# Nine buffers of widened counts in place of six, and a quarter of GpSimd's descriptor ring, in a three-layer graph network on one Trainium2 core

## The chip, the cores and the metric

The kernel runs on one core of one Trainium2 chip. The metric is the device time of one execution in microseconds (us). The kernel before takes 7069.22 us, the median of three runs (7048.0 to 7079.48).

## What is computed

12500 nodes of 128 features, 200000 edges sorted by destination. The first layer is a gated one: messages of the source nodes plus an embedding of the edge's type are summed at their destinations, and a GRU cell updates the nodes. Three layers follow in which each node sums its neighbours' rows and encoded edge attributes, and a two-layer perceptron with a batch norm turns the sums. Each half ends in a layer norm of the residual.

```python
def _gin_layer(x, ei, ea, p, concat):
    enc_w, enc_b, w1, b1, g, be, rm, rv, w2, b2 = p
    ee = ea @ enc_w + enc_b
    src = x[ei[1]]
    h = jnp.concatenate([src, ee], axis=1) if concat else src + ee
    agg = jax.ops.segment_sum(h, ei[0], num_segments=x.shape[0])
    h = agg @ w1 + b1
    h = jax.nn.relu(_bn_eval(h, g, be, rm, rv))
    return h @ w2 + b2
...
x = _layernorm(x + _L0_gnn_ref(x, edge_index, edge_type_9, ...), axis=-1)
x = _layernorm(x + _L1_gnn_ref(x, edge_index, edge_attr_16, ...), axis=-1)
```

`_L1_gnn_ref` calls `_gin_layer` three times, with a self loop added for every node.

## The kernel before, in words

The program has three stages, one after the other, on five queues that its author wrote out by hand: TensorE, VectorE, ScalarE, GpSimd and SP (which issues the plain DMAs). There is no scheduler. Each instruction waits for a count on a semaphore, and each engine takes its instructions in the order in which they are written.

**Sorting and counting.** The edges are ranked and written to memory in a new order by 1563 scatters of GpSimd (L3017, one DMA of 128 records each). For the destinations in groups of 512 and the first 60 blocks of 128 source nodes (60 is `BD`), one-hot matrices are multiplied into matrices of counts: how many edges lead from source s to destination d. The counts are bytes and lie in memory (`counts`).

**First layer.** It has counted blocks and gathered blocks; 611 gathers of GpSimd fetch rows (L3033), into 16 buffers (`QR`) of four tiles each. Its output goes to memory in two forms, as dense parts (for the counted blocks) and as rows to gather.

**Three layers.** 25 groups of 512 destinations in each, so 75 groups k (`SG` is 25; the last group of nodes has 256). The 60 counted source blocks of a group are taken in 30 steps (`HALF`) of two blocks each. For a step:

- SP loads counts, two steps at a time, 256 KB into one of five buffers of `MS` (`MR` = 5, L3248). Before it reuses a buffer, it waits until both widenings of it are done.
- ScalarE (L2575) or, every third step, VectorE (L2258) widens 128x1024 bytes to 32-bit floats in one of `RM` buffers of `MSR`. Before that it waits until the step that used this buffer before has been multiplied (`m_used`, a semaphore that TensorE raises with the last matmul of a step). The widening of step g is written four steps ahead (`AH` = 4) of step g's place in these engines' programs.
- TensorE (L2965) does four matmuls: two blocks, each with a high and a low part of the node features (`HP`), against the widened counts, and adds all into one PSUM bank. It waits for the step's widening.

The sources that aren't counted are gathered: GpSimd fetches their rows (L3051) into six buffers of `GL`, VectorE makes one-hots (L2239), TensorE sums (L2935), VectorE adds three parts up (L2276, L2269) and TensorE turns the result (L2880, L2884). There are 28 gathers in a group. Between the steps of group k stand the perceptron's pieces for group k - 1 (L2899 to L2914 on TensorE, L2295 and L2302 on VectorE, L2610 to L2638 on ScalarE), and SP loads and stores what they need. At the end of a layer, SP reloads `HP` in pieces of 2 MB, 2 MB, 3 MB and 0.5 MB (L3251), and the count loads of the next group stand behind these in its queue.

What the change touches are the number of buffers `RM`, with the waits and the index in L2256 to L2259, L2573 to L2576 and L2965, and the size of the area in which GpSimd's DMAs (L3017, L3033, L3051) keep their descriptors. The tensors start behind that area. The wait of a widening is

```python
            if g >= RM:
                s.wait_ge(m_used.sem, g - RM + 1)
```

Of the kernel before, what the change touches and what calls it, by code (L numbers as in the profile page):

```python
# [48 lines left out]
BD = 4 * J  # L49
HALF = 2 * J  # L50
MR = 5
RM = 6
AH = 4
HB = [0, 16, 32, BD - 4, BD]
NQ0 = (C + GT - 1) // GT
# [1503 lines left out]
def program(nc, x, dst, src, typ, ea, wmsgT, wihT, whhT, emb, bmsg, bih, bhh, encT, w1a, w1b, w2, pv, out):  # L1559
    ctx = ExitStack()  # L1560
    with ctx:
        def sb(name, shape, dt=F32, into=ctx):
            return into.enter_context(nc.sbuf_tensor(name, shape, dt))
# [154 lines left out]
        MS = sb("MS", [P, MR, 1024], BF16, layers)  # L1718
        MSR = sb("MSR", [P, RM, 2, 512], F32R, layers)
        GL = sb("GL", [P, LR, LT, 448], BF16, layers)  # L1720
# [531 lines left out]
        def widen_vector(v, g):  # L2252

            i, w = g // 2, GRP[g // HALF].w
            v.wait_ge(m_in[i % MR].sem, 16 * (i // MR + 1))
            if g >= RM:  # L2256
                v.wait_ge(m_used.sem, g - RM + 1)
            v.tensor_copy(MSR[:, g % RM, :, 0:w].rearrange("p t (c s) -> p t c s", s=P),  # L2258
                          MSB[:, i % MR, 0:4 * w].rearrange("p (c h s t) -> p h t c s", h=2, s=P, t=2)[:, g % 2]).then_inc(*wide_dve.inc())  # L2259
# [309 lines left out]
        def widen_scalar(s, g):  # L2569

            i, w = g // 2, GRP[g // HALF].w
            s.wait_ge(m_in[i % MR].sem, 16 * (i // MR + 1))
            if g >= RM:  # L2573
                s.wait_ge(m_used.sem, g - RM + 1)
            s.copy(MSR[:, g % RM, :, 0:w].rearrange("p t (c s) -> p t c s", s=P),  # L2575
# [884 lines left out]
```

## Time and profile before

| | us |
|---|---|
| median of 3 runs | 7069.22 |
| lowest, highest run | 7048.0, 7079.48 |
| span of the profiled execution | 6981.5 |
| TensorE busy in it | 5386.3 (77%) |
| GpSimd busy | 4213.9 (60%) |
| VectorE busy | 3769.9 (54%) |
| ScalarE busy | 3302.5 (47%) |

The profile is of one execution. For this one only the span, from the first to the last instruction, is listed; what lies around it is not. An engine's busy time is the union of its instructions; a matmul's end is modelled, its start is recorded. The granted clock is TensorE's as a share of the full one. "Idle before" is the time for which an engine did nothing just before an instruction, put down to what ended it; "remote" and "another core or an unknown queue" are waits for which the profile found no releaser, "issue" is time in which it saw no wait.

### The profile page before, as it was taken

How to read it: one execution, taken by the hardware profiler on the slowest of the kernel's cores; microseconds unless marked ns; L12 is line 12 of the kernel's file. 1: busy time of each engine (PE TensorE's matmuls, PEld its weight loads, DVE VectorE, ACT ScalarE, POOL GpSimd, SP SyncE). 2: the span in 40 equal slices, each digit the busy share in tenths (PEclk: the TensorE clock that was granted, in tenths of full speed). 3: DMA queues.
4: the chain of work that ended last, by engine and by line, in shares of the span. 5: the costliest groups of instructions: out<-in, count | busy, mean ns of one | idle time of the engine just before them, and what ended most of it. 6: DMA issues, size and time to landing. Idle time of an engine off the chain costs nothing.

```text
span 6981.5 us, 88118 instructions
## 1 busy us (share of the span) xinstructions
PE 5386.3 (77%) x26429; PEld 3361.9 (48%) x26429; DVE 3769.9 (54%) x14165; ACT 3302.5 (47%) x4432; POOL 4213.9 (60%) x4243
## 2 busy tenths in 40 slices
PE   4376767676766764666676999999898998898998
PEld 1133333333333322333344666666666666666666
DVE  8576767777766754455566444443333333444443
ACT  1164545555655641122122666665555554554554
POOL 5655555555555556666631666666676666666665
PEclk5588988888988985677776999999999999999999
DMA  7165556556655652333323666667666667666665
GB/s 250 48 144 129 140 121 138 127 134 136 157 127 127 148 138 76 98 101 102 100 78 121 188 190 185 194 196 220 184 186 179 190 191 217 184 184 174 177 185 148
DMA packets 1068177, 1066.40 MB, mean 153 GB/s; under 512 B 494051, under 2 KB 784501, under 8 KB 1067701
## 3 DMA queue, kind: packets, MB, share of 16 engines
q1 hardware_dynamic: 889573, 782.05, 40.1%
q0 software_dynamic: 178128, 278.65, 16.0%
q8 instruction: 220, 3.60, 0.2%
q14 instruction: 256, 2.10, 0.1%
HBM read 747.21 MB, written 216.68 MB: 138 GB/s over the span
## 4 chain that ended last, share of the span: by engine, by line
PE 44%; another core or an unknown queue 6%; DVE 4%; issue 4%; ACT 2%; DMA 1%; SPq 0%; DVEq 0%; ACTq 0%
PE ps L2965 27%; PE ps L2935 4%; PE ps L2848 2%; PE ps L2899 2%; PE ps L2809 2%; PE ps L2810 1%; DVE BIG L2197 1%; PE ps L2909 1%; PE ps L2910 1%; PE ps L2811 1%; ACT MSR L2575 1%; DVE MSR L2258 0%; PE ps L2812 0%; PE ps L2914 0%
## 5 line engine op out<-in xcount | busy, mean ns | idle before, releaser
L3051 POOL DMA_INDIRECT GL<-h_gathered,IDXA x2058 | 2112.6, 1027 | 1227.7 <-issue 568.5
L2965 PE MATMUL ps<-MSR,HP 128*128 128x512 f32 (+1 forms) x9000 | 2375.0, 410 | 174.9 <-ACT MSR L2575 71.2
L3017 POOL DMA_INDIRECT rec_q<-BIG x1563 | 1513.7, 968 | 1156.2 <-issue 473.6
L2575 ACT CAST MSR<-MS 128x1024 fp32r<-128x1024 uint8 (+1 forms) x1500 | 1491.8, 1028 | 1272.9 <-PE ps L2965 820.3
L2965 PEld LDWEIGHTS ps<-MSR,HP 128*128 128x128 f32 x9000 | 1675.6, 195 | 624.9 <-issue 168.5
L2750 PE MATMUL ps<-MTB,XPS 128*128 128x512 bf16 x4410 | 1312.2, 416 | 1.1 <-DMA XPS<-x_parts 0.8
L2258 DVE CAST MSR<-MS 128x1024 fp32r<-128x1024 uint8 (+1 forms) x750 | 522.6, 699 | 1236.7 <-PE ps L2965 738.5
L2457 ACT CAST MT<-ps 128x512 uint16<-128x512 f32 x735 | 427.4, 582 | 959.2 <-remote 633.3
L2461 ACT CAST MTB<-MT 128x1024 bf16<-128x1024 uint8 x735 | 767.9, 1045 | 64.8 <-PE ps L2750 10.3
L3033 POOL DMA_INDIRECT BIG<-x_parts,SRCq x611 | 582.8, 954 | 341.5 <-issue 164.4
L2750 PEld LDWEIGHTS ps<-MTB,XPS 128*128 128x128 bf16 x4410 | 439.7, 103 | 248.7 <-issue 68.1
L2935 PE MATMUL ps<-GL,SL 128*128 128x384 bf16 (+1 forms) x2058 | 456.0, 338 | 8.9 <-issue 7.3
L2709 PE MATMUL ps<-BIG 128*128 128x392 f16 x435 | 165.2, 380 | 354.4 <-DVE BIG L2052 269.1
L2733 PE MATMUL ps<-BIG 128*128 128x256 bf16 x738 | 215.5, 293 | 286.8 <-DVE BIG L2034 83.7
L2034 DVE TENSOR_SCALAR BIG<-I,BIG 128x258 bf16<-128x258 f16 x982 | 335.0, 399 | 188.3 <-remote 162.5
L2197 DVE TENSOR_SCALAR BIG<-IO,DREL 128x256 bf16<-128x256 f16 x1579 | 352.7, 299 | 94.2 <-remote 84.6
L2239 DVE TENSOR_SCALAR SL<-IOTH,RELA 128x128 bf16<-128x128 f16 x2058 | 387.1, 263 | 0.0
L1976 DVE TENSOR_SCALAR BIG<-IOTM,BIG 128x98 f16<-128x98 f16 x1804 | 346.5, 254 | 0.0
L2809 PE MATMUL ps<-WE,BIG 10*128 10x512 f32 x196 | 166.3, 940 | 197.7 <-ACT XMT L2522 158.8
L2052 DVE CAST BIG<-ps 128x98 f16<-128x98 f32 x435 | 109.6, 252 | 306.9 <-remote 288.0
L2733 PEld LDWEIGHTS ps<-BIG 128*128 128x128 bf16 x738 | 77.6, 105 | 395.7 <-issue 179.7
L2935 PEld LDWEIGHTS ps<-GL,SL 128*128 128x128 bf16 x2058 | 154.7, 98 | 229.3 <-issue 166.2
(248 smaller groups left out, 6244.4 us busy)
## 6 DMA issues: line engine op xcount, KB each, us to landing
MS<-counts SPq DMA_DIRECT2D x1080, 256.0 KB
counts<-BIG SPq DMA_DIRECT2D x360, 256.0 KB
XPS<-x_parts SPq DMA_DIRECT2D x192, 384.0 KB
GL<-h_gathered,IDXA POOLq DMA_INDIRECT x2058
rec_q<-BIG POOLq DMA_INDIRECT x1563
rec_q<-BIG SPq DMA_DIRECT2D x44, 490.0 KB, 10.4
HTI<-h_cols SPq DMA_DIRECT2D x72, 256.0 KB
h_dense<-PCL SPq DMA_DIRECT2D x30, 512.0 KB
```

Source lines behind the costliest of these rows:

```text
L2197: got = v.tensor_scalar(hot[:, i, :], IO256[:, :], DREL[:, GT * q + i:GT * q + i + 1], None, ALU.is_equal)
L2239: got = v.tensor_scalar(SL[:, r % LR, i, :], IOTH[:, :], RELA[:, q + i:q + i + 1], None, ALU.is_equal)
L2258: v.tensor_copy(MSR[:, g % RM, :, 0:w].rearrange("p t (c s) -> p t c s", s=P), MSB[:, i % MR, 0:4 * w].rearrange("p (c h s t) -> p h t c s ...
L2457: s.copy(MT[:, m % 3, 512 * i:512 * (i + 1)].bitcast(U16), PS[PAIR[(p0 + i) % 2]][:, :]).then_inc(*mt_out.inc())
L2461: s.copy(MTB[:, m % 3, 1024 * i:1024 * (i + 1)], MT[:, m % 3, 512 * i:512 * (i + 1)].bitcast(U8)).then_inc(*mtb.inc())
L2575: s.copy(MSR[:, g % RM, :, 0:w].rearrange("p t (c s) -> p t c s", s=P), MSB[:, i % MR, 0:4 * w].rearrange("p (c h s t) -> p h t c s", h=2, ...
L2750: got = t.matmul(PS[6 + x.j % 2][:, :], XPS[:, x.load % 3, i, part, :], MTB[:, m % 3, 512 * i:512 * (i + 1)], start=4 * x.u + i + part == ...
L2935: got = t.matmul(bank[:, 0:w], SL[:, r % LR, i, :], GL[:, r % LR, i, 0:w], start=at + i == 0, stop=at == 1 and i == TS[1] - 1, skip_group_ ...
L2965: got = t.matmul(bank[:, 0:w], HP[:, d, part, :], MSR[:, g % RM, d % 2, 0:w], start=d + part == 0, stop=lay > 0 and d + part == BD, skip_g ...
L3017: g.indirect_dma_start(out=RAd, out_offset=bass.IndirectOffsetOnAxis(ap=POSI[:, c:c + 1], axis=0), in_=RECA[q % 3][:, c - a, :], in_offset ...
L3033: g.indirect_dma_start(out=XG[:, r % QR, i, 0:3 * P], out_offset=None, in_=XPd, in_offset=bass.IndirectOffsetOnAxis(ap=SRCi[:, GT * q + i: ...
L3051: g.indirect_dma_start(out=GL[:, r % LR, i, 0:3 * P], out_offset=None, in_=HGd[lay], in_offset=bass.IndirectOffsetOnAxis(ap=IDXA[:, a + i: ...
```

## The change

The widened counts get nine buffers in place of six. Each buffer takes 4 KB of a partition (two blocks of 512 floats), so three more take 12 KB. The same room is taken from the area for the descriptors of GpSimd's DMAs, which is set to 4096 bytes of each partition; by the name of the change that is a quarter of what it was.

```diff
@@ -49,7 +49,7 @@
 BD = 4 * J
 HALF = 2 * J
 MR = 5
-RM = 6
+RM = 9
 AH = 4
 HB = [0, 16, 32, BD - 4, BD]
 NQ0 = (C + GT - 1) // GT
@@ -3448,7 +3448,7 @@
     import concourse.bacc as bacc
     from concourse.bass_utils import run_bass_kernel_spmd
 
-    nc = bacc.Bacc("TRN2", target_bir_lowering=False, num_devices=1)
+    nc = bacc.Bacc("TRN2", target_bir_lowering=False, num_devices=1, dynamic_dma_scratch_size=4096)
     arrays, args = {}, []
     for name, a in _layout({k: np.asarray(a) for k, a in inputs.items()}).items():
         arrays[f"in_{name}"] = a
```

The instructions of all five queues are the same and stand in the same order. What differs in them is the buffer's number and the count for which a widening waits.

## Rows read from the trace of the kernel before

**Rows 1.** The page: the span.
```profile
span 6981.5 us, 88118 instructions
```

**Rows 2.** First and third stage: us; busy PE, PEld, DVE, ACT, POOL; clock, DMA, GB/s.
```profile
0.00:2675.00 2675.00, 1733.68 (x9600) 871.09 (x9600) 1854.91 (x7086) 1286.73 (x1714) 1518.12 (x1574) 0.81 0.56 135
...
3803.00:6981.50 3178.50, 2913.09 (x12596) 2062.15 (x12596) 1279.52 (x3919) 1772.60 (x2141) 2112.64 (x2058) 0.96 0.65 189
```

**Rows 3.** The page's groups: busy us, mean ns of one, idle us before.
```profile
L3051 POOL DMA_INDIRECT GL<-h_gathered,IDXA x2058 | 2112.6, 1027 | 1227.7 <-issue 568.5
L2965 PE MATMUL ps<-MSR,HP 128*128 128x512 f32 (+1 forms) x9000 | 2375.0, 410 | 174.9 <-ACT MSR L2575 71.2
...
L2575 ACT CAST MSR<-MS 128x1024 fp32r<-128x1024 uint8 (+1 forms) x1500 | 1491.8, 1028 | 1272.9 <-PE ps L2965 820.3
...
L2258 DVE CAST MSR<-MS 128x1024 fp32r<-128x1024 uint8 (+1 forms) x750 | 522.6, 699 | 1236.7 <-PE ps L2965 738.5
```

**Rows 4.** Waits of the third stage: total us, times, longest.
```profile
ACT MSR L2575 <- PE ps L2965: 820.3, 501, 8.8
DVE MSR L2258 <- PE ps L2965: 738.5, 270, 10.5
...
PE ps L2965 <- ACT MSR L2575: 71.2, 35, 16.9
PE ps L2965 <- issue: 70.1, 61, 7.3
PE ps L2880 <- DVE MM L2276: 35.1, 13, 5.6
PE ps L2965 <- DVE MSR L2258: 18.2, 17, 2.8
PE ps L2965 <- DMA HP<-h_dense: 14.4, 2, 8.2
```

**Rows 5.** Timeline of TensorE, 6617 to 6630: start, us, what, idle before.
```profile
6617.48 2.12 PE L2965 MATMUL ps<-MSR,HP 128*128 128x512 f32 x8
...
6627.48 2.81 PE L2965 MATMUL ps<-MSR,HP 128*128 128x512 f32 x11 [2.00 <-ACT MSR L2575]
```

**Rows 6.** The same stretch on ScalarE.
```profile
6621.43 1.05 ACT L2575 CAST MSR<-MS 128x1024 fp32r<-128x1024 uint8 x1 [3.94 <-issue]
...
6626.39 3.90 ACT L2575 CAST MSR<-MS 128x1024 fp32r<-128x1024 uint8 x4 [3.71 <-PE ps L2965]
```

**Rows 7.** Timeline of all engines, 6454 to 6461.
```profile
6454.06 0.94 DVE L2258 CAST MSR<-MS 128x1024 fp32r<-128x1024 uint8 x1 [7.38 <-remote]
...
6455.06 2.08 PE L2965 MATMUL ps<-MSR,HP 128*128 128x512 f32 x4 [4.40 <-issue]
...
6459.68 4.84 ACT L2575 CAST MSR<-MS 128x1024 fp32r<-128x1024 uint8 x5 [10.25 <-remote]
...
6460.78 2.07 PE L2965 MATMUL ps<-MSR,HP 128*128 128x512 f32 x4 [3.64 <-ACT MSR L2575]
```

**Rows 8.** Timelines at the two reloads of node parts, 4872 and 5936.
```profile
4872.68 18.55 SPq L3248 DMA_DIRECT2D MS<-counts  x7
...
4888.87 3.36 PE L2965 MATMUL ps<-MSR,HP 128*128 128x512 f32 x7 [9.79 <-ACT MSR L2575]
...
5936.73 1.65 PE L2965 MATMUL ps<-MSR,HP 128*128 128x512 f32 x3 [7.27 <-issue]
```

**Rows 9.** Stage windows: a stretch without stalls, one with two.
```profile
4100.00:4200.00 100.00, 97.56 (x428) 66.97 (x427) 44.43 (x137) 65.23 (x92) 68.52 (x67) 1.00 0.65 184
...
6450.00:6500.00 50.00, 41.23 (x165) 28.70 (x164) 18.25 (x58) 21.74 (x24) 30.07 (x30) 0.86 0.58 157
```

**Rows 10.** GpSimd's DMAs: durations min/median/max in ns, and its waits.
```profile
L3017 POOL DMA_INDIRECT rec_q<-BIG x1563: 952/958/1733, 22.7 to 2674.4; - x196
...
POOL rec_q L3017 <- issue: 473.6, 1350, 4.6
POOL rec_q L3017 <- DMA rec_q<-BIG: 260.7, 139, 4.9
```

## The prediction

> **What bounds the kernel now.** I read the page first, then stage windows, groups by line, waits, and timelines around single stalls. The execution has a span of 6981.5 us [rows 1], and by the table no engine is busy for the whole of it. The stage windows cut it in three: sorting and counting (2675 us), the first layer (the 1128 us between), and the three last layers (3178.5 us) [rows 2]. The tiles that the change enlarges live only in the third stage; its descriptor ring is used in all three.
>
> In the third stage TensorE is busy 2913.1 of 3178.5 us, 92%, at a mean granted clock of 0.96 [rows 2]. So TensorE bounds it, and each us in which it stands still counts. Its largest group is L2965, 9000 matmuls of node parts by widened counts, 2375.0 us busy with 174.9 us idle in front [rows 3]. A step is four of them, on one buffer of MSR: 2250 steps, 3178.5 / 2250 = 1.41 us each, 2913.1 / 2250 = 1.29 us where nothing stands. GpSimd gathers for 2112.6 us, with 568.5 us of issue between, and waits for others in the rest [rows 3]; ScalarE and VectorE are far from full.
>
> Who waits for whom: ScalarE's widening waits 820.3 us for L2965 to free a buffer, VectorE's 738.5 us [rows 4]. That is idle time of engines that have time. But TensorE in turn waits before L2965 for ScalarE's widening (71.2 us), for VectorE's (18.2 us) and 70.1 us for what the profile can't name [rows 4]. The question is why a widening is late when its engine stands idle.
>
> One stall shows it. At 6626.39 ScalarE begins the widening of step 25 of a group, after 3.71 us of idling that a signal of L2965 ended [rows 6]. With six buffers it needs the buffer of step 19. That step's matmuls are the last of the eight begun at 6617.48, over at 6619.60 by the profile [rows 5]. So the signal came 6.8 us after them, and not alone: the row is one of four widenings without a pause, each of which needed a later signal [rows 6]. TensorE had finished step 24 by 6625.48 and stood 2.00 us [rows 5]. The loads were not late: the load of that pair of steps had served the widening at 6621.43 already.
>
> So the buffers are freed in time and **the news of it comes late, in bunches**. Six buffers are 6 x 1.29 = 7.7 us of work, and part of that goes on the widening itself (1.05 us). Rows 4 count 113 waits of TensorE's before L2965 of this kind, 159.5 us in all. The longest pair stands in [rows 7]: TensorE is out of work at 6450.66 (4.40 us before 6455.06), VectorE's widening comes at 6454.06, TensorE does one step more, and ScalarE's comes at 6459.68 after 10.25 us of idling; 8.04 us are lost.
>
> The Trainium skill ("TensorE: Matmul & The Clock Gate", section "The cost: per-tile semaphore tail") has each increment of a semaphore by a matmul cost some 26 ns, one after the other. By that rule the news would be there at once; the 6.8 us above disagree with it, and if it held where no profile is taken, there would be no gain (rival two).
>
> **The change, part by part.** No instruction moves on any of the five queues; a constant in a wait and an index change.
>
> (1) *Nine buffers.* Widening g now waits for step g-9, not g-6. Program order still puts it four steps ahead of its use, so this bites only where an engine runs ahead of TensorE, as both do [rows 4]. In the stall above the widenings of steps 25, 26 and 27 need steps 16, 17 and 18, all signalled by 6621.43, so TensorE has three more steps, 3 x 1.29 = 3.9 us, and the 2.00 us are covered. Terms:
> - idle before L2965: 174.9 us [rows 3];
> - less what is no buffer's fault: 16.9 us at the stage's start (the longest wait for ScalarE), 14.4 us for node parts [rows 4], and 9.79 and 7.27 us where the count load stands behind a 3 MB reload of the node parts (issued at 4872.68, just behind L3251's; TensorE goes on at 4888.87) [rows 8]: leaves 126.5 us;
> - less the parts of long stalls beyond 3.9 us, and stalls where the engine itself was occupied: I take a fifth off, 100 us left;
> - TensorE's clock: the stage's mean is 0.96, so it loses 0.04 x 3178.5 = 127 us of full speed. A stretch without stalls runs at 1.00, one with two long ones at 0.86 [rows 9]: the lower of the two levels (1.2 GHz) comes with and after standing still. The stalls that go are about half of the stage's idle time (265 us [rows 2]); since part of each slow stretch is the stall itself, I take a third of 127: 40 us.
>
> Together 140 us gross. What is late next: the same late signals hold up other waits that nine buffers don't touch, the sums of gathered rows on VectorE above all (TensorE waits 35.1 us for L2276 at L2880) [rows 4]. VectorE takes its instructions in order, and a row sum that waits for a late signal holds the next widening behind it, however many buffers there are. Against that, a widening that doesn't wait holds up nothing behind it either. I take 0.6 of the gross: **85 us gain**. Bounds of this term: 0 (every stall becomes one of the other waits) and 126.5 + 64 (half of the clock's loss) = 190 us. Below nothing I see no way: the new wait is for an earlier event.
>
> The instructions that widen are the same, so their 1.03 and 0.70 us stay [rows 3]; count loads (five in flight, untouched) can be issued a little earlier, never later.
>
> (2) *A quarter of the ring.* It costs GpSimd something only if the room runs out. How many of its DMAs are in flight? It issues one in 0.96 + 473.6 / 1350 = 1.3 us [rows 10]; the longest that a scatter waited for the landing of earlier ones is 4.9 us [rows 10], and there at least one more was issued in between, so a DMA lands within some 7 us: 6 in flight. The ring before must have held more than that, since 1563 scatters have a median of 958 ns and a maximum of 1733, with no sign of waiting for room. I cost it at **nothing**; the cover is the landing time, and if it is gone, each DMA beyond the room waits for the oldest to land. Bounds: 0, and one landing of 3 us at each time around the ring (rival three).
>
> The Trainium skill speaks against this part. "SBUF — State Buffer" ("SBUF size: 192, 224, or 256?") gives the ring 16 KiB of a partition, and "DMA: Bandwidth & Descriptors" ("The descriptor swizzle") nine descriptors on each side and engine for such a DMA, of 16 bytes each. An estimate from these pages: 4096 / 16 / 9 = 28 DMAs in the small ring where 113 were. No row shows a ring's size. By these pages the room would be ample and the sum the same.
>
> **Sum.** 6981.5 - 85 + 0 = 6896.5 us of span. The page lists no more of the profiled execution than its span; the median of the three runs, 7069.2, is 87.7 us above it, and I carry these over unchanged: **6984 us**, 1.2% faster. I call over 0.5%, 35 us, the least that a measurement of this kernel can tell from no change.
>
> **Rivals.**
> *One: the whole gross gain.* If the row sums aren't in the way, the 140 us stay: 6930 us. For it: no other wait of TensorE's shown for the stage is above 36 us [rows 4]. Against: bunches hold all of TensorE's signals.
> *Two: no change.* A late signal is late because TensorE stands or is about to, or VectorE's queue is blocked by the row sums, so the stall only moves three steps on; or the late signals belong to the profiled execution alone. For it: both signals of the longest pair came 3.4 and 2.5 us after TensorE's last matmul, when it stood [rows 7]. Against: ScalarE's widening at 6621.43 had waited 3.94 us for step 18, over at 6618.7, and TensorE worked all the time [rows 5, 6]. Then 10 to 25 us remain of the gain: 7050 us.
> *Three: slower, by the ring.* GpSimd, on reaching the end of its ring, waits until what is in flight has landed, and does so four times as often. A landing wait is 260.7 / 139 = 1.9 us for a scatter after one more issue of 1.3 us: 3.2 us [rows 10]. A round is unknown from rows; between the 6 in flight and the 64 gathers that the first layer's buffers let run ahead I take 20. The 2174 DMAs of the first two stages then make 109 rounds, 82 of them new: 262 us, of which 0.74 lie on the path as far as GpSimd is occupied there (1518.1 us busy and 473.6 us of issue in 2675 [rows 2, 10]): 194 us, and 7069 - 85 + 194 = 7178 us. The third stage has GpSimd time to spare. It decides from rounds of 32 DMAs down, where 51 new rounds cost 120 us, the gain and 35 us more. Against: scatters of 952 ns at least and 958 in the median show no wait in the large ring [rows 10]. With the 28 DMAs that come out of the two pages of the Trainium skill, it would be 137 us and 7121 us.
> That the ring never fills to nine, so that the change does nothing, is rival two again.
>
> **How the numbers follow.** Forecast (6940 to 7030): 0.48. Rival one: 0.14. Rival two: 0.28. Rival three: 0.10. Faster by over 0.5%: nearly all of the first two: 0.61. Same: rival two and a little of the forecast: 0.29. Slower: 0.10. The range takes rival one with the larger bound of the clock term at its low end, 6900, and rival two with a disturbed first stage at its high end, 7085; beyond it lie the far end of the bound (6879) and rival three.
>
> **What would show it.** Right: idle before L2965 falls from 174.9 to 60 to 90 us, what is left being the start and the reloads; the widenings' waits for L2965 fall by hundreds of us; granted clock of the last stage 0.97 or 0.98; that stage some 85 us shorter, the first two within 5 us; the scatters' median of 958 ns unchanged. Wrong: the same idle under another name (L2880, L2899), the widenings waiting for "remote" as long as before, or longer DMA_INDIRECT rows in the first 2675 us.

## The result, and the profile after

| | before | after |
|---|---|---|
| median, 9 runs each | 7079.48 us | 7124.39 us |
| lowest, highest | 7048.0, 7098.91 | 7108.05, 7151.58 |
| ratio, 95% interval | | 1.0065 (1.0042 to 1.0089) |
| profiled execution: time, span | -, 6981.5 | 7139.66, 7137.1 |

The change makes the kernel slower by 45 us, or 0.65%; the forecast was 6984 us and faster. Some 3 us lie around the span (7139.66 - 7137.1), not the 87.7 us that the prediction carried over. The three runs of before that gave 7069 and its profiled execution seem not to belong together: in four of the five sessions below (a session is a group of runs taken together on one chip) the same kernel has medians of 6970 to 6990 us, in one 7076, and its span of 6981.5 fits the four. So the traces of before and after differ by the session too, and the lengths of stages are compared below mainly between kernels of one session. What the engines wait for can be compared, with a margin: a second trace of the kernel before (e4) has other amounts.

The page's groups of the kernel after, which answer to [rows 3], with the scatters of [rows 10] (busy us, mean ns of one, idle us before and its main releaser):

```profile
L3051 POOL DMA_INDIRECT GL<-h_gathered,IDXA x2058 | 2094.3, 1018 | 1305.6 <-issue 567.4
L2965 PE MATMUL ps<-MSR,HP 128*128 128x512 f32 (+1 forms) x9000 | 2380.9, 411 | 97.6 <-issue 52.8
L3017 POOL DMA_INDIRECT rec_q<-BIG x1563 | 1509.5, 966 | 1232.2 <-issue 453.7
...
L2575 ACT CAST MSR<-MS 128x1024 fp32r<-128x1024 uint8 (+1 forms) x1500 | 1463.6, 1027 | 778.2 <-PE ps L2965 481.4
...
L2258 DVE CAST MSR<-MS 128x1024 fp32r<-128x1024 uint8 (+1 forms) x750 | 517.5, 699 | 447.4 <-PE ps L2965 211.9
```

At the place where they stand, the nine buffers do what was said of them. The widenings' idle time falls from 1272.9 and 1236.7 us [rows 3] to 778.2 and 447.4, and the idle time before L2965 from 174.9 to 97.6. The stage windows (as [rows 2], with the first layer between):

```profile
0.00:2749.00 2749.00, 1701.03 (x9419) 866.12 (x9600) 1855.12 (x7090) 1283.90 (x1714) 1514.27 (x1574) 0.80 0.55 132
2749.00:3910.00 1161.00, 742.89 (x4233) 428.88 (x4233) 637.38 (x3159) 244.37 (x579) 593.70 (x621) 0.69 0.33 92
3910.00:7137.00 3227.00, 2927.97 (x12596) 2077.30 (x12596) 1252.41 (x3918) 1732.95 (x2141) 2085.09 (x2049) 0.96 0.63 185
```

But TensorE stands in the last stage for 3227.0 - 2928.0 = 299 us, where it was 265 [rows 2], and the granted clock is still 0.96. Where it stands now is in the waits of TensorE from 3910 to 7137 (total us, times, longest), beside [rows 4]:

```profile
PE ps L2880 <- DVE MM L2276: 57.1, 19, 5.9
PE ps L2965 <- issue: 52.8, 81, 6.7
PE ps L2880 <- issue: 38.8, 17, 6.5
PE ps L2884 <- DVE MM L2274: 29.9, 7, 5.0
PE ps L2965 <- ACT MSR L2575: 26.1, 3, 16.8
PE ps L2914 <- ACT HTO L2621: 25.8, 15, 5.8
PE ps L2935 <- issue: 21.9, 34, 1.8
```

Before L2880, the turning of the row sums, TensorE waits 96 us (57.1 and 38.8). The groups by line of the kernel before, for the same places:

```profile
L2276 DVE TENSOR_REDUCE MM<-ps 128x128 f32<-128x384 f32 x196 | 108.7, 555 | 202.6 <-remote 98.0 <-PE ps L2935 77.5 <-issue 26.9
L2880 PE MATMUL ps<-IDN,MM 128*128 128x128 f32 x196 | 56.4, 288 | 39.7 <-DVE MM L2276 35.1 <-issue 4.5
L2914 PE MATMUL ps<-IDN,HTO 128*128 128x128 f32 x294 | 45.3, 276 | 2.6 <-ACT HTO L2621 2.6
L2884 PE MATMUL ps<-IDN,MM 128*17 128x128 f32 x98 | 27.3, 279 | 20.9 <-issue 10.9 <-DVE MM L2274 9.8
```

and of the kernel after:

```profile
L2276 DVE TENSOR_REDUCE MM<-ps 128x128 f32<-128x384 f32 x196 | 108.4, 553 | 603.0 <-remote 377.7 <-PE ps L2935 137.0 <-issue 88.1
L2880 PE MATMUL ps<-IDN,MM 128*128 128x128 f32 x196 | 57.2, 292 | 96.1 <-DVE MM L2276 57.1 <-issue 38.8
L2914 PE MATMUL ps<-IDN,HTO 128*128 128x128 f32 x294 | 46.7, 282 | 28.9 <-ACT HTO L2621 25.8 <-issue 2.9
...
L2884 PE MATMUL ps<-IDN,MM 128*17 128x128 f32 x98 | 27.9, 285 | 45.5 <-DVE MM L2274 29.9 <-issue 15.5
```

L2880, L2884 and L2914 gained 56.4, 24.6 and 26.3 us of idle time, 107 us together, where L2965 lost 77. These amounts are of one pair of traces. In the second traces of the two kernels (e4 and f3 below) L2965 has 148.9 and 112.7 us, the three other lines 82 and 129: it loses 36 and they gain 47. The direction is the same, the sizes are not firm. VectorE now stands idle before its row sum L2276 for 603.0 us, not 202.6. One such stall in the timeline of the kernel after, from 5698 to 5712 (start, us, what, idle before):

```profile
5698.94 0.66 PE L2935 MATMUL ps<-GL,SL 128*128 128x384 bf16 x3
...
5699.30 3.97 PE L2965 MATMUL ps<-MSR,HP 128*128 128x512 f32 x16
...
5708.54 0.56 DVE L2276 TENSOR_REDUCE MM<-ps 128x128 f32<-128x384 f32 x1 [11.33 <-remote]
5708.65 3.88 ACT L2575 CAST MSR<-MS 128x1024 fp32r<-128x1024 uint8 x4 [0.50 <-remote]
5708.78 1.04 POOL L3051 DMA_INDIRECT GL<-h_gathered,IDXA  x1 [2.49 <-remote]
5709.02 1.29 DVE L2258 CAST MSR<-MS 128x1024 fp32r<-128x1024 uint8 x2
...
5709.15 0.48 PE L2880 MATMUL ps<-IDN,MM 128*128 128x128 f32 x1 [5.89 <-DVE MM L2276]
```

TensorE is out of work at 5703.27 and stands, since L2880 is next in its order and needs the row sum. The matmuls that sum the gathered rows are over at 5699.60 (5698.94 + 0.66, an end that is modelled). VectorE has been idle for 11.33 us when the row sum starts; 8.9 of them come after that end. VectorE, ScalarE and GpSimd, each of which waits for TensorE here, go on within 0.24 us of one another (5708.54 to 5708.78): that is the bunch. L2880 starts 0.61 us after the row sum does; the widening of VectorE comes right behind it. It is the late signal of the prediction, at a wait that nine buffers don't touch.

The kernel before has the same late signal, and there TensorE stands in two places for it. Its timeline from 5398 to 5412:

```profile
5399.49 0.66 PE L2935 MATMUL ps<-GL,SL 128*128 128x384 bf16 x3
...
5406.56 2.08 PE L2965 MATMUL ps<-MSR,HP 128*128 128x512 f32 x4 [3.34 <-issue]
...
5411.11 0.56 DVE L2276 TENSOR_REDUCE MM<-ps 128x128 f32<-128x384 f32 x1 [8.65 <-remote]
...
5411.73 0.47 PE L2880 MATMUL ps<-IDN,MM 128*128 128x128 f32 x1 [3.09 <-DVE MM L2276]
```

The row sum starts 11.0 us after the matmuls of 5399.49 are over. TensorE stands 3.34 us for a widened buffer and 3.09 us for the row sum; in the kernel after it stands 5.89 us, all of it for the row sum. This fits a stall that has moved: with more buffers TensorE gets to the row sum's place, and the signal is late there too. The two stalls are of different groups, so they show the pattern and not a size.

Two questions were open: what the smaller ring costs, and what the buffers bring by themselves.

### The profile page after: what moved, and what is told of

Same layout as the page of the kernel before. It is cut to its first block, busy times and chain, and to the rows that moved or that the text cites. A ratio compares the mean times of both kernels' runs of the same rounds, so it can differ in the third digit from the quotient of the medians.

```text
span 7137.1 us, 87934 instructions
## 1 busy us (share of the span) xinstructions
PE 5371.9 (75%) x26248; PEld 3372.3 (47%) x26429; DVE 3744.9 (52%) x14165; ACT 3261.2 (46%) x4432; POOL 4193.1 (59%) x4243
## 3 DMA queue, kind: packets, MB, share of 16 engines
q0 software_dynamic: 178128, 278.65, 15.6%
## 4 chain that ended last, share of the span: by engine, by line
PE 45%; DVE 23%; another core or an unknown queue 19%; issue 7%; ACT 3%; DMA 2%; SPq 1%; DVEq 0%; ACTq 0%
PE ps L2965 23%; PE ps L2935 4%; PE ps L2750 3%; DVE BIG L2034 3%; DVE BIG L1976 3%; DVE BIG L2053 2%; PE ps L2848 2%; DVE BIG L2065 2%; DVE BIG L2028 2%; PE ps L2809 2%; PE ps L2899 2%; DVE WE L2034 2%; PE ps L2810 1%; PE ps L2733 1%
## 5 line engine op out<-in xcount | busy, mean ns | idle before, releaser
L2965 PE MATMUL ps<-MSR,HP 128*128 128x512 f32 (+1 forms) x9000 | 2380.9, 411 | 97.6 <-issue 52.8
L2965 PEld LDWEIGHTS ps<-MSR,HP 128*128 128x128 f32 x9000 | 1695.0, 196 | 530.7 <-issue 150.2
L2575 ACT CAST MSR<-MS 128x1024 fp32r<-128x1024 uint8 (+1 forms) x1500 | 1463.6, 1027 | 778.2 <-PE ps L2965 481.4
L2750 PE MATMUL ps<-MTB,XPS 128*128 128x512 bf16 x4229 | 1255.1, 411 | 14.3 <-issue 5.2
L3033 POOL DMA_INDIRECT BIG<-x_parts,SRCq x611 | 584.5, 957 | 361.2 <-issue 169.6
L2258 DVE CAST MSR<-MS 128x1024 fp32r<-128x1024 uint8 (+1 forms) x750 | 517.5, 699 | 447.4 <-PE ps L2965 211.9
L2935 PE MATMUL ps<-GL,SL 128*128 128x384 bf16 (+1 forms) x2058 | 463.2, 339 | 22.5 <-issue 21.9
L2276 DVE TENSOR_REDUCE MM<-ps 128x128 f32<-128x384 f32 x196 | 108.4, 553 | 603.0 <-remote 377.7
L2239 DVE TENSOR_SCALAR SL<-IOTH,RELA 128x128 bf16<-128x128 f16 x2058 | 390.1, 262 | 0.0
L2935 PEld LDWEIGHTS ps<-GL,SL 128*128 128x128 bf16 x2058 | 155.1, 99 | 245.9 <-issue 184.8
```

The costliest lines, as they stand in the source:

```text
L2750: got = t.matmul(PS[6 + x.j % 2][:, :], XPS[:, x.load % 3, i, part, :], MTB[:, m % 3, 512 * i:512 * (i + 1)], start=4 * x.u + i + part == ...
L2935: got = t.matmul(bank[:, 0:w], SL[:, r % LR, i, :], GL[:, r % LR, i, 0:w], start=at + i == 0, stop=at == 1 and i == TS[1] - 1, skip_group_ ...
L2965: got = t.matmul(bank[:, 0:w], HP[:, d, part, :], MSR[:, g % RM, d % 2, 0:w], start=d + part == 0, stop=lay > 0 and d + part == BD, skip_g ...
L3033: g.indirect_dma_start(out=XG[:, r % QR, i, 0:3 * P], out_offset=None, in_=XPd, in_offset=bass.IndirectOffsetOnAxis(ap=SRCi[:, GT * q + i: ...
```

## The experiments

All edits below are against the kernel before, unless it says "after". Ratios are to the kernel before, timed in the same session. The first session has e1 to e4 (before: 6969.81 us), the second f1 to f4 (7076.19), the third g1 to g4 (6974.97), the fourth h1 to h4 (6990.33), the last i1 and i2 (6978.19).

**e1: the small ring alone.**

```diff
-    nc = bacc.Bacc("TRN2", target_bir_lowering=False, num_devices=1)
+    nc = bacc.Bacc("TRN2", target_bir_lowering=False, num_devices=1, dynamic_dma_scratch_size=4096)
```

> Six buffers, a quarter of the descriptor ring, every tensor 12 KB lower. Ring theory (the small ring costs GpSimd or the DMAs something): all of the loss and more, since the nine buffers took idle time away: ratio 1.010 to 1.015, first matmul of L2965 some 60 to 95 us later than at 3815 us, scatters longer or their waits for landing longer. Address theory (it is where the tensors lie): the same ratio, here not told apart. Buffer theory (nine buffers themselves cost): ratio 1.000, within 0.3%. Scatter theory (the trace of before was a fast one, the first stages differ by chance): first L2965 anywhere between 3815 and 3910, ratio 1.000.

7063.11 us, ratio 1.0115 (1.0083 to 1.0147).

**e2: the same, with the addresses of before.** An unused tensor fills the 12 KB.

```diff
+        PADR = sb("PADR", [P, 3072])
```

> As the one before, with an unused tensor of 12 KB in front of all others, so that every tensor lies where it lay before and only the ring is small. Ring theory: as the run with the ring alone, 1.010 to 1.015. Address theory: 1.000. Buffer theory and scatter theory: 1.000.

7020.97 us, ratio 1.007 (1.0039 to 1.0101). It is slower with the addresses of before too, so these aren't the whole cause. Whether they are part of the 42 us between e1 and e2 is not clear here, as the two intervals overlap; h3 and h4 repeat the pair.

**e3: room for nine buffers, but the wait of six**, with the ring of 4096.

```diff
-RM = 6
+RM = 9
+RW6 = 6
...
-            if g >= RM:
-                s.wait_ge(m_used.sem, g - RM + 1)
+            if g >= RW6:
+                s.wait_ge(m_used.sem, g - RW6 + 1)
```

> The changed kernel with room for nine buffers, small ring, but a widening waits for step g - 6 as before. Ring or address theory: slower than the changed kernel, since what the late signals cost is back: 1.010 to 1.015. Buffer theory (widening further ahead is what costs): back to 1.000. Idle before L2965 rises from 97.6 us to about 175 us in either case.

7046.44 us, ratio 1.0102 (1.0069 to 1.0134): within e1's interval, as it should be if the room alone does nothing. The idle time before L2965 is 148.2 us, not 175, but no more is due: e1 has 142.4.

**e4: the kernel before, unchanged.**

> The kernel before, for a second trace. Ratio 1.000 within 0.3%. If the first trace (span 6981.5, while the median of nine runs is 7079.5) was a lucky one, the span is now 7050 to 7095 us, and the first L2965 starts at 3840 to 3900 us; if it stays near 6980, the runs beside it are what is odd.

6985.15 us, ratio 1.0003 (0.9977 to 1.003). Its profiled execution took 7016.17 us and is the slowest of its twelve; L2965 starts at 3840 us. Its line of L2965, beside that of [rows 3] with 174.9:

```profile
L2965 PE MATMUL ps<-MSR,HP 128*128 128x512 f32 (+1 forms) x9000 | 2382.2, 411 | 148.9 <-issue 63.5
```

So two traces of one kernel differ by 26 us in this idle time. Over all the traces with six buffers but g2 it is 142 to 187 us, and with eight or nine 90 to 113 (g1 apart).

**f1, f2: rings of 2048 and 8192 bytes**, six buffers, with the line of e1.

> Six buffers, ring of 2048 bytes of a partition, half of the changed kernel's. Ring theory with a price for each round of the ring (rounds twice as many as with 4096): twice the loss of the ring alone (1.0115), 1.02 to 1.03. Ring theory with a threshold (something that fits in the large ring and not in 4096): at least 1.010, a jump if the DMAs in flight no longer fit. Address theory (what matters is where the tensors lie; they move by 2 KB more): anything, 1.000 to 1.012, no order by size.

7123.49 us, ratio 1.0061 (1.0035 to 1.0087).

> Six buffers, ring of 8192 bytes, twice the changed kernel's. Price for each round: a third of the loss of 4096 (rounds two times those of 16384 in place of four times: one extra unit against three), 1.003 to 1.005. Threshold: 1.000 or 1.010. Address theory: no order.

7110.79 us, ratio 1.0059 (1.0028 to 1.0091). Both are slower than before and by the same, with four times as many rounds in one as in the other. That is neither a price for each round nor a threshold as they were expected. The scatters of f1, by the source line (ns least, median, most):

```profile
L3017 POOL DMA_INDIRECT rec_q<-BIG x1563: 952/959/1734, 22.7 to 2759.2; - x196
```

and of the kernel after:

```profile
L3017 POOL DMA_INDIRECT rec_q<-BIG x1563: 952/958/1736, 22.7 to 2746.1; - x196
```

The ring is an eighth of the first in one, a quarter in the other, and the median and the longest are within 3 ns of those of before (958 and 1733). No row shows GpSimd waiting for room. In the traces of before, after and the small rings I found at most 5 of its DMAs in flight when the next is issued, counted from their issues and the packets of their queue. The stage of scatters ends at 2769 us in f1 and at 2709 in f2. With one trace each that decides nothing: h3 and h4, which have one size of ring, are 38 us apart there.

**f3: the kernel after, again.**

> The changed kernel again, on the chip of these runs. If ring (1.0115 and 1.010) and nine buffers are two separate terms: 1.004 to 1.008, below the kernel with the ring alone, the difference being what the nine buffers gain, 0.3 to 0.6%. If the nine buffers gain nothing: 1.010.

7086.4 us, ratio 1.0015 (0.999 to 1.004). Against f1 and f2 of the same session it is 0.3 to 0.5% faster. None of f1 to f4 has six buffers with the ring of 4096. In its trace the idle time before L2965 is 112.7 us, before L2880 87.8.

**f4: eight buffers, ring of 8192.** With one wait more between two stages, which is long met.

```diff
-RM = 6
+RM = 8
...
+            y.wait_ge(idx_made.sem, 2 * (NS // IX))
```

> Eight buffers and a ring of 8192 bytes (one wait is added at the start of the three layers, for a semaphore that GpSimd waits for there too, so that tensors which now share other places don't meet). If both terms are real and the ring's goes by rounds: +0.4% for the ring, -0.4% for two more buffers: 1.000, within 0.3%. If the ring has a threshold between 4096 and 8192: 0.996. If neither: 1.000.

7083.23 us, ratio 1.0016 (0.9988 to 1.0043). The same ring with six buffers (f2) took 7110.79: two more buffers are worth 27.6 us or 0.4% by the medians, though the two intervals overlap. In its trace L2965 waits for 90.4 us, L2880 for 76.9.

**g1, g2: the turning of the row sums four steps of its order later**, in the kernel after (g1) and in the kernel before (g2).

```diff
-    return 4 * (ROW_AT[2 * c + 1] + 1) - 1 + 8
+    return 4 * (ROW_AT[2 * c + 1] + 1) - 1 + 12
```

> The changed kernel, with TensorE's turning of the row sums (L2880, L2884) written four blocks, two steps, later. Moved-wait theory (nine buffers took about 70 us of idle time from in front of L2965, and the late signals of L2935 put as much in front of L2880 and L2884, since VectorE's row sum comes late): idle before L2880 falls from 88 to 96 us to under 50, and the last stage is 20 to 50 us shorter than the changed kernel's (3179 to 3207 us): ratio 0.998 or below. If the idle time before L2880 isn't what holds the nine buffers back (it comes back before another line): as the changed kernel, 1.0015 to 1.0065.

6997.5 us, ratio 1.0024 (0.9999 to 1.005). The wait before L2880 fell as expected, the time did not.

> The kernel before with the same later turning: the control. Moved-wait theory: with six buffers the stalls stand before L2965, so only the 40 us or so before L2880 can go: 0.997 to 1.000. If turning later helps either kernel equally, the pair says nothing for nine buffers.

6995.51 us, ratio 1.0032 (1.0006 to 1.0057), where 0.997 to 1.000 was expected. With six buffers the later turning doesn't help either: in the trace L2880 waits for 1.4 us, and L2965 for 220.6. The two lines of TensorE in the groups of g1:

```profile
L2965 PE MATMUL ps<-MSR,HP 128*128 128x512 f32 (+1 forms) x9000 | 2372.6, 410 | 176.8 <-issue 119.2 <-DVE MSR L2258 37.8 <-DMA HP<-h_dense 15.6
...
L2880 PE MATMUL ps<-IDN,MM 128*128 128x128 f32 x196 | 55.6, 284 | 2.6 <-issue 2.6
```

The wait at L2880 is gone (96.1 to 2.6) and stands before L2965 again (97.6 to 176.8, about the 174.9 of six buffers). VectorE still sits at the row sum, and its own widening, behind it in program order, now comes late: `DVE MSR L2258` ends 37.8 us of it, 3.1 us in the kernel after; most of the rest (119.2) has no named releaser. Taking away one place where the late signal hurts makes another, in either kernel.

Not all of it comes back, though. L2965, L2880, L2884 and L2914 together stand 202 us in g1, 268 in the kernel after and 242 in f3. The last stage of g1 is 3155 us long, the shortest of all the traces, with a granted clock of 0.97. In time g1 and g2 are level (6997.5 and 6995.51), although g1 has the small ring. If that costs some 50 us, as h1 to h4 say, then nine buffers with the later turning are worth about as much. That is an estimate: no run here has both with the whole ring.

**g3: the ring 1 KB smaller**, 15360 bytes, and 1 KB of unused tensor, so that all addresses are as before.

> Six buffers, ring of 15360 bytes in place of 16384, with 1 KB unused behind it, so that all tensors lie as before. Theory that any ring but that of 16384 costs (8192 and 2048 cost the same 0.6%): 1.006. Size theory (the cost sets in between 8192 and 16384, by the room): 1.000. Scatter theory (a kernel's runs differ by build as much as that): anything in 0.996 to 1.006.

7007.23 us, ratio 1.0043 (1.0014 to 1.0071): even this came out slower, in a single run of this size and with no harmless edit beside it. After it, sizes of 2048, 4096, 8192 and 15360 bytes had cost 0.61, 0.7 to 1.15, 0.59 and 0.43%: no order but that all are slower. g2, whose ring is whole, was slower too, so "any other build of this kernel is slower" explained as much as "a smaller ring is slower".

**g4: gathers of 16 rows.** The three layers' gathers fetch 16 rows of 128, so 112 rows of each are left out; the buffers are cleared once.

```diff
-                                out=GL[:, r % LR, i, 0:3 * P], out_offset=None, in_=HGd[lay],
-                                in_offset=bass.IndirectOffsetOnAxis(ap=IDXA[:, a + i:a + i + 1], axis=0)).then_inc(*rows_in[r % LR].inc(16))
+                                out=GL[0:16, r % LR, i, 0:3 * P], out_offset=None, in_=HGd[lay],
+                                in_offset=bass.IndirectOffsetOnAxis(ap=IDXA[0:16, a + i:a + i + 1], axis=0)).then_inc(*rows_in[r % LR].inc(16))
```

> Six buffers, large ring; in the three layers each of GpSimd's 2058 gathers fetches 16 rows in place of 128, the other rows are zeros, and VectorE clears the tile once. Same number of DMAs, of waits and of matmuls, an eighth of the descriptors and bytes. If TensorE's late signals come from the traffic of GpSimd's descriptors or of the gathered rows: the idle time before L2965 (175 us) falls below 80 us and the last stage by 80 us and more, ratio 0.985. If they have nothing to do with it: L2965's idle time within 30 us of before, ratio 0.997 to 1.002.

7054.83 us, ratio 1.0105 (1.0056 to 1.0153). The longest wait of L2276 for an unnamed signal is still 8.8 us:

```profile
DVE MM L2276 <- remote: 168.2, 37, 8.8
```

The idle time before L2965 is 173.8 us, that of before, and this is the row sum of the longest wait: it starts 7.1 us after the matmuls before it (6212.02 + 0.66) are over. (L2940 is L2935 in this kernel's numbering.)

```profile
6212.02 0.66 PE L2940 MATMUL ps<-GL,SL 128*128 128x384 bf16 x3
...
6219.78 0.56 DVE L2276 TENSOR_REDUCE MM<-ps 128x128 f32<-128x384 f32 x1 [8.76 <-remote]
```

So the amount of gathered rows doesn't make the late signals. Why the kernel is slower, no run here tells.

**h1 to h4: a smaller ring, or any other build?** h1 moves most tensors by 512 bytes and leaves the ring alone; h2 adds only the wait of f4; h3 is e2 again, h4 is e1 again.

```diff
+        PADR = sb("PADR", [P, 128])
```

> The ring is left at its default and six buffers, an unused tensor of 512 bytes per partition stands ahead of the others, so that most tensors move by 512 bytes and not one instruction changes. Theory A (a smaller ring of GpSimd's descriptors costs by itself): nothing changes, ratio 0.998 to 1.002. Theory B (the kernel of before stands at a favourable point of its timing, and any other build of it is slower): 1.003 or more.

7001.24 us, ratio 1.0005 (0.9986 to 1.0024).

> The ring and the six buffers of before, with one wait added on SyncE between the stages, on a count that is long complete there. Theory A (the smaller ring costs): 0.998 to 1.002. Theory B (any other build is slower): 1.003 or more.

6997.46 us, ratio 0.9999 (0.9979 to 1.002).

> Six buffers, ring of 4096 bytes, every tensor at its address of before: the same kernel as e2, on another chip and in the same call as h1 and h2. Theory A (ring): 1.004 or more, and clearly above h1 and h2. Theory B (any other build): about the same as h1 and h2.

7050.91 us, ratio 1.0084 (1.0058 to 1.0111).

> Six buffers, ring of 4096 bytes and nothing else, the same kernel as e1. Theory A (ring): 1.006 to 1.012, as e1, and not far from h3. Theory B (any other build): somewhere from 1.003 to 1.012, within the spread of h1, h2 and h3. If it comes out under 1.003, the 1.0115 of e1 was a matter of the chip or the run, and the price of the ring is smaller than e1 says.

7049.15 us, ratio 1.0079 (1.0052 to 1.0106). The intervals of the two pairs lie well apart. **The ring of 4096 bytes costs 0.8% by itself**: 59 and 61 us against the kernel before, 48 to 53 against h1 and h2. These two other builds cost nothing, and h3 and h4 are alike, so no effect of the addresses shows. The windows of the first layer (from its first gather to the first widened matmul), for h1:

```profile
2692.00:3835.00 1143.00, 747.12 (x4233) 431.36 (x4233) 636.17 (x3159) 243.96 (x578) 591.44 (x621) 0.69 0.33 93
```

for h2:

```profile
2689.00:3833.00 1144.00, 744.38 (x4238) 430.35 (x4239) 638.94 (x3183) 244.50 (x579) 591.27 (x621) 0.69 0.33 93
```

for h3:

```profile
2659.00:3811.00 1152.00, 741.97 (x4233) 428.65 (x4233) 635.02 (x3158) 243.63 (x579) 593.80 (x621) 0.69 0.32 93
```

and for h4:

```profile
2697.00:3846.00 1149.00, 739.62 (x4233) 428.77 (x4233) 634.79 (x3157) 244.22 (x578) 592.69 (x621) 0.70 0.32 93
```

That layer is 5 to 9 us longer with the small ring, with GpSimd 1 to 3 us busier, and no other engine busier than in the slower of h1 and h2. The last stage is 3198 and 3183 us (7009 - 3811, 7029 - 3846) where h1 and h2 have 3177 and 3182. The stage of 1563 scatters isn't longer at all (2659 and 2697 against 2692 and 2689). That is some 18 us of the 50; the profiled execution of h3 was the fastest of its six (7012.03 against a median of 7050.91), so a single trace can't show the rest.

Over all the traces the first layer is what differs most steadily. The same window takes 1137 to 1147 us in the eight with the whole ring, 1148 with 15360 bytes (g3) and 1149 to 1168 in the ten with 4096 or 8192. GpSimd's idle time before the gathers of that layer (L3033) is 337 to 347 us in the eight, 343 in g3 and 352 to 365 in the ten. But f1, with 2048 bytes, has 1144 and 351 us and is as slow as f2. The packets of GpSimd's queue take the same share of the DMA engines' time, 15.6 and 15.5% in h1 and h2, 15.6% in h3 and h4. So the cost has no one place that was found, and no engine's wait carries its name.

**i1, i2: more buffers with the whole ring.** The room comes from the gathered rows, four batches in place of six. i1 has eight buffers of counts; i2, the control, has six.

```diff
-LR = 6
+LR = 4
...
-RM = 6
+RM = 8
```

> Eight buffers of widened counts with the ring at its default: the room comes from the buffers of gathered rows and their one-hots, four batches in place of six. The widenings' gaps should fall to about 1550 us as in f4 (eight buffers, ring of 8192 bytes: ratio 1.0016). If the small ring is what costs and more buffers are worth some 0.4%, this kernel comes out faster than before, 0.994 to 0.998. If the buffers are worth nothing by themselves, or the four batches of gathered rows hold up the row sums, it comes out at 1.000 or above.

6991.01 us, ratio 0.9998 (0.9971 to 1.0026): level with the kernel before, not faster. The widenings' gaps are 817 us (625.0 and 191.9), not 1550.

> The control of i1: six buffers, default ring, four batches of gathered rows in place of six. If the four batches cost nothing (GpSimd stands idle for 1228 us of the last stage, and a batch of four gathers takes it about 4 us), ratio 0.998 to 1.002, and i1 stands below it by the worth of two more buffers. If they do cost, this is above 1.002, and i1 is to be read against this one.

7033.84 us, ratio 1.0079 (1.0056 to 1.0103). So two more buffers are worth 42.8 us or 0.6% with the ring whole, and two batches fewer of gathered rows and one-hots cost 0.8%. The groups of i1:

```profile
L2965 PE MATMUL ps<-MSR,HP 128*128 128x512 f32 (+1 forms) x9000 | 2372.2, 410 | 107.0 <-issue 63.7
...
L2258 DVE CAST MSR<-MS 128x1024 fp32r<-128x1024 uint8 (+1 forms) x750 | 506.7, 682 | 191.9 <-PE ps L2965 90.0
...
L2239 DVE TENSOR_SCALAR SL<-IOTH,RELA 128x128 bf16<-128x128 f16 x2058 | 400.4, 267 | 1467.0 <-remote 744.9
```

and of i2:

```profile
L2965 PE MATMUL ps<-MSR,HP 128*128 128x512 f32 (+1 forms) x9000 | 2381.1, 411 | 147.6 <-issue 64.2
...
L2258 DVE CAST MSR<-MS 128x1024 fp32r<-128x1024 uint8 (+1 forms) x750 | 517.6, 693 | 724.1 <-PE ps L2965 475.6
...
L2239 DVE TENSOR_SCALAR SL<-IOTH,RELA 128x128 bf16<-128x128 f16 x2058 | 403.6, 267 | 1015.6 <-remote 445.3
```

The idle time before L2965 is 40.6 us apart. That it is about the gain in the medians is chance in part: L2880, L2884 and L2914 wait for 147 us in i1 and 131 in i2, and i1's profiled execution is the slowest of its twelve, i2's the fastest of its six. VectorE's wait has moved too. With four batches its one-hots (L2239) wait for earlier sums of gathered rows, 1015.6 us in i2 and 1467.0 in i1, where the kernel before has none; the widenings stand behind them in VectorE's order. In i1 L2880 still waits 66.0 us for the row sums, in i2 43.5:

```profile
PE ps L2880 <- DVE MM L2276: 66.0, 25, 5.1
```

No kernel here beats the one before.

## Why the prediction was wrong

**Step (1), nine buffers: mechanism right, size too large.** The idle time before L2965 was to fall to 60 to 90 us; it fell to 97.6, in f3 to 112.7. The saving there was put at 100 us and is 77 against the first trace, 36 from e4 to f3. Two terms after it failed as well.
- *"TensorE's clock: 40 us."* The granted clock of the last stage is 0.96 in the kernels before and after, and 0.95 to 0.97 in the others. It was to rise because TensorE would stand less; TensorE stands 299 us of the last stage after and 265 before, so nothing was given back.
- *"I take 0.6 of the gross."* The prediction named the row sums as what is late next, and costed them at 0.4 of 140 us. By the traces L2880, L2884 and L2914 took 107 us where L2965 gave 77. By the times, which count, two more buffers gave 27.6 us (f4 against f2) and 42.8 us (i1 against i2), and nine with a small ring 24 and 37 us (f3 against f2 and f1, whose rings have other sizes). So the term is some 25 to 45 us where 85 stood: between the forecast and rival two, whose remaining gain was put at 10 to 25. The sign of being wrong that the prediction gave, the same idle time before L2880, came.

The prediction had the reason: VectorE's row sum waits for the same late signals. It priced it too low. The row sum can't start before the late signal, whatever the widening does. Before, VectorE spent part of that time waiting for a buffer (738.5 us [rows 4]); when that wait goes, it reaches the row sum sooner and waits there (L2276: 98.0 to 377.7 us for "remote"), and TensorE stands behind it. g1 and g2 show the same from the other side. That signals are late only while a profile is taken, the other half of rival two, no run here tests.

**Step (2), "I cost it at nothing": failed, and it decided the sign.** h1 to h4 put it at 0.8%. The cover that I named seems to be there: at most 5 DMAs in flight, no row with a wait for room, and scatters of 958 ns as before. Neither the rows nor anything that the prediction drew on names what it costs instead.

The Trainium skill's figures ("SBUF — State Buffer", section "SBUF size: 192, 224, or 256?", and "DMA: Bandwidth & Descriptors", section "The descriptor swizzle") gave, as an estimate, room for 28 DMAs; 5 in flight agree with a room that doesn't run out, but no row shows a ring's size.

I had made "the room runs out" the only way for a small ring to cost anything. A part whose mechanism isn't seen in any row deserved a range on the side of slower, and only rival three had one, with 0.10.

**Rival three** has the right sign for the wrong reason. It needs more rounds of the ring to cost more, and 2048 bytes cost no more than 8192 or 4096; the scatter stage, with 1563 of the 4232 DMAs, would have had to show it first, and isn't longer in h3 and h4.

**The sum.** Buffers -0.4% to -0.6% and ring +0.8% make +0.2% to +0.4%. The kernel after has 1.0065 in one session and 1.0015 in another; the two intervals (1.0042 to 1.0089, 0.999 to 1.004) don't quite touch. That difference stays unexplained. e1 (1.0115) and h4 (1.0079), which are the same kernel, have intervals that overlap.

**The 87.7 us between span and median** were most likely a comparison of two sessions. They did no harm to the saving, since they were taken from and added to the same sum, but no run shows such a term: 2 to 5 us lie around the span in every run whose span is listed.

**Still open:** by what a smaller ring slows the kernel. Ruled out are addresses (e2, h3) and that a new build costs in itself (h1, h2); against waits for room speak the durations of GpSimd's DMAs, also with 2048 bytes (f1). Nor does any run show why TensorE's signals come late. Not tried was a ring larger than the first, for which the room would have to come from other buffers.

## What to carry to other kernels

When one signal is late for several engines, a deeper buffer at one of its waits moves the stall to the next: list every wait on that signal and look which comes next in the order of the engine that bounds, before pricing a buffer. Of the idle time that went from before the widened matmuls, a third to a half came back in the time of f3 and f4 against f1 and f2 (68 to 90 us of idle time, 24 to 37 us of time), and about all of it in i1 against i2 (41 and 43).

A setting whose use no trace shows (here the area for descriptors) isn't free just because nothing shows it full. Change it alone, with the addresses held by a pad, beside a harmless edit and the unchanged kernel in the same session: before h1 and h2 stood beside them, kernels with four sizes of ring didn't tell a ring's cost from a build's.

A profiled execution is one draw from runs that lie up to 1% to one side, and its session another; below 1% use traces for who waits for whom, with a second trace of the same kernel beside the first, and medians of one session for how much.

## What the runs showed of the hardware

- In these traces signals of TensorE reach other engines late and in bunches: a row sum of VectorE starts 11.0 us (before), 8.9 us (after) and 7.1 us (g4, with an eighth of the gathered rows) after the modelled end of the matmuls that it waits for, where the prediction had seen 6.8 us at a widening. In the second of these, three engines go on within 0.24 us of one another.
- A smaller area for GpSimd's descriptors costs time though no row shows a wait for room: 4096 bytes cost 0.70 to 1.15% in four kernels of two sessions, 0.8% beside two controls without cost. 2048, 8192 and 15360 bytes came out at 0.61%, 0.59% and 0.43%, each in one kernel with no such control in its session.
- One kernel, unchanged, has medians from 6969.81 to 7079.48 us over the sessions, 1.6% apart, more than any edit here moves it by. Two of them, 7076.19 and 6974.97, are of one chip, 22 minutes apart.
